# A first expert layer whose weights become the loaded operand, in a decoder layer on one core

## The reference

```python
for e in range(E):                                   # E = 4 experts, F = 512
    g = silu(einsum('bsd,fd->bsf', hidden_states, Wg[e]))
    u = einsum('bsd,fd->bsf', hidden_states, Wu[e])
    y = einsum('bsf,df->bsd', g * u, Wd[e])
    out = where((expert_ids == e)[..., None], y, out)
```

## Time and profile before

| what | value |
|---|---|
| median of 3 runs | 975.06 us (973.46 to 976.2) |
| profiled execution, its own time | 981.35 us |
| its span | 979.6 us |
| TensorE products / operand loads | 916.6 us busy / 517.6 us busy |
| VectorE, ScalarE, GpSimd busy | 698.2, 616.4, 325.2 us |
| expert and quantised stage | from 733.7 us to the end |

### The profile page before, as it was taken

How to read it: one execution, slowest core, us unless ns; L and a number is a source line. 1 busy time by engine, 2 the same in 40 slices (tenths; PEclk the granted TensorE clock), 3 DMA queues, 4 the chain that set the end, 5 groups by cost and what they waited for, 6 DMA issues and landing times.

```text
span 979.6 us, 19017 instructions
## 1 busy us (share of the span) xinstructions
PE 916.6 (94%) x6525; PEld 517.6 (53%) x6540; DVE 698.2 (71%) x1533; ACT 616.4 (63%) x1570; POOL 325.2 (33%) x450
## 2 busy tenths in 40 slices
PE   3899999999999999999999999999949899999974
PEld 2366676556556655655656556566414344444331
DVE  6799978778876778777667766776543378777672
ACT  3777778677777766776767667664102279887552
POOL 3477867123231422433242222301330012322211
PEclk9899999999999999999999999999978999999998
DMA  9636546676975534655454434459859977444343
GB/s 245 156 87 138 119 98 121 161 187 180 194 183 162 131 96 110 137 131 114 100 104 107 108 98 124 98 134 191 205 145 190 185 136 146 97 98 97 76 107 87
DMA packets 305631, 131.86 MB, mean 135 GB/s; under 512 B 275264, under 2 KB 279872, under 8 KB 305536
## 3 DMA queue, kind: packets, MB, share of 16 engines
q1 hardware_dynamic: 301616, 117.77, 56.0%
q0 software_dynamic: 3920, 12.86, 3.9%
HBM read 42.76 MB, written 20.99 MB: 65 GB/s over the span
## 4 chain that ended last, share of the span: by engine, by line
PE 82%; DMA 4%; DVE 3%; SPq 2%; issue 2%; ACT 2%; POOL 0%; DVEq 0%; ACTq 0%; POOLq 0%
PE S L250 7%; PE S L252 7%; PE S L251 7%; PE O L596 6%; PE QB L250 6%; PE QB L251 6%; PE QB L252 6%; PE O L594 5%; PE O L598 5%; PE OUTB L250 5%; PE OUTB L251 5%; PE OUTB L252 5%; PE OUTB L714 4%; PE S L698 4%; DMA P<-QTOKR 2%
## 5 line engine op out<-in xcount | busy, mean ns | idle before, releaser
L596 PE MATMUL O<-V,P 128*128 128x128 f16 x1024 | 179.1, 221 | 0.0
L594 PE MATMUL O<-V,P 128*128 128x129 f16 x1024 | 179.0, 219 | 0.1
L598 PE MATMUL O<-V,P 128*128 128x129 f16 x1024 | 178.9, 218 | 0.0
L1134 DVE CAST P<-P 128x1024 bf16<-128x1024 f32 x128 | 92.5, 723 | 113.5 <-ACT P L813 113.4
L1136 DVE TENSOR_TENSOR P<-P 128x1024 f16<-128x1024 f32 x128 | 161.0, 1258 | 4.4
L813 ACT ACTIVATE P<-S,cst 128x1024 f32<-128x1024 f32 x128 | 142.6, 1114 | 27.6 <-PE S L252 27.6
L1461 POOL TENSOR_SCALAR qst<-qs 128x4 f32<-128x4 f32 x64 | 14.2, 221 | 348.9 <-ACT junk L796 348.9
L796 ACT ACTIVATE junk<-QB 128x128 bf16<-128x128 f32 x208 | 54.6, 277 | 103.3 <-PE QB L252 103.3
L824 ACT ACTIVATE OTOK<-O,rd 128x128 f16<-128x128 f32 x256 | 80.5, 375 | 40.7 <-DVE rd L1141 40.0
L596 PEld LDWEIGHTS O<-V,P 128*128 128x128 bf16 x1024 | 99.2, 97 | 7.3
L594 PEld LDWEIGHTS O<-V,P 128*128 128x128 bf16 x1024 | 98.5, 96 | 7.9 <-DVE P L1136 0.6
(11 more groups left out here) (225 smaller groups left out, 1957.2 us busy)
## 6 DMA issues: line engine op xcount, KB each, us to landing
SIDE<-in_L_ffn_w_dram SPq DMA_DIRECT2D x64, 256.0 KB, 3.2
OTA<-sorted_rows SPq DMA_DIRECT2D x4, 1028.0 KB, 7.7
OTA<-in_L_attn_Wq_dram SPq DMA_DIRECT2D x4, 1024.0 KB, 6.9
SIDE<-in_L_attn_Wout_dram SPq DMA_DIRECT2D x16, 256.0 KB, 3.4
SIDE<-in_ctx_dram SPq DMA_DIRECT2D x16, 256.0 KB
ctx_split<-SIDE SPq DMA_DIRECT2D x16, 256.0 KB, 3.1
ROWB<-in_x_dram SPq DMA_DIRECT2D x16, 256.0 KB, 3.2
w_tern<-SIDE SPq DMA_DIRECT2D x32, 128.0 KB, 3.0
```

Source lines behind the costliest of these rows:

```text
L594: nc.tensor.matmul(o, ph(g)[:, a:a + P], V[:, b % 2, j, 0:129], start=j == 0, stop=False)
L596: nc.tensor.matmul(o[:, 0:128], ph(g)[:, a:a + P], V[:, b % 2, j, 130:258], start=False, stop=False)
L598: last = nc.tensor.matmul(o, pl(g)[:, a:a + P], V[:, b % 2, j, 0:129], start=False, stop=j == NT - 1)
L1134: nc.vector.tensor_copy(ph(g)[:, cols], P32[:, cols]).then_inc(p_hi, 1)
```

## The change

up() swaps the operands: a block of 128 features of the expert's weights is the loaded operand, and the tile's 128 turned rows are streamed past it. The product comes out with features on partitions and tokens in columns, block f in columns f * 128 of the same half of O. The gated values are then written straight to GT, and turn_gated, GHL and the semaphores gt fall away. gated_high now waits for the down() that read its part of GT four pairs ago (y_ps), and down() waits for gated_low (gu_lo).

```diff
-        GHL = (QTOKR[:, 0, :], QTOKR[:, 1, :])
...
-            def turn_gated(j):
-                sp.wait_ge(gu_lo, j + 1)
-                if j >= 4:
-                    sp.wait_ge(y_ps, j - 3)
-                sp.dma_start_transpose(GT[:, j % 4, :].rearrange("p (a n) -> p a n", n=P),
-                                       GHL[j % 2]).then_inc(gt[j % 4], 16)
-
...
-                if j < PAIRS:
-                    turn_gated(j)
...
+            def expert_block(e, s_, c, f):
+                return CT[:, bass.ds(e * 4096 + (s_ * DC + c) * F + f * P, P)]
+
+
             def up(j):
...
-                for c in range(DC):
-                    lhs = [HT[:, bass.ds(t * 1024 + (s_ * DC + c) * P, P)] for s_ in range(2)]
-                    last = split_products(O[:, (j % 2) * 512:(j % 2 + 1) * 512], lhs[0], lhs[1],
-                                          expert_rows(e, 0, c), expert_rows(e, 1, c), c == 0, c == DC - 1)
+                for f in range(F // P):
+                    for c in range(DC):
+                        rows = [HT[:, bass.ds(t * 1024 + (s_ * DC + c) * P, P)] for s_ in range(2)]
+                        a = (j % 2) * 512 + f * P
+                        last = split_products(O[:, a:a + P], expert_block(e, 0, c, f), expert_block(e, 1, c, f),
+                                              rows[0], rows[1], c == 0, c == DC - 1)
                 last.then_inc(z_ps, 1)
 
             def down(j):
                 e = pe.value_load(table[0:1, bass.ds(j, 1)], min_val=0, max_val=E - 1)
-                pe.wait_ge(gt[j % 4], (j // 4 + 1) * 16)
+                pe.wait_ge(gu_lo, j + 1)
...
             def gated_high(j):
                 act.wait_ge(gu, j + 1)
-                if j >= 2:
-                    act.wait_ge(gt[j % 4 - 2], ((j - 2) // 4 + 1) * 16)
-                nc.scalar.activation(GHL[j % 2][:, 0:F].bitcast(BF16), GU[j % 2], ACT.Copy
-                                     ).then_inc(gu_hi, 1)
+                if j >= 4:
+                    act.wait_ge(y_ps, j - 3)
+                nc.scalar.activation(GT[:, j % 4, 0:F].bitcast(BF16), GU[j % 2], ACT.Copy).then_inc(gu_hi, 1)
...
             def gated_low(j):
                 dve.wait_ge(gu_hi, j + 1)
-                nc.vector.tensor_tensor(GHL[j % 2][:, F:2 * F], GU[j % 2],
-                                        GHL[j % 2][:, 0:F].bitcast(BF16), ALU.subtract).then_inc(gu_lo, 1)
+                nc.vector.tensor_tensor(GT[:, j % 4, F:2 * F], GU[j % 2], GT[:, j % 4, 0:F].bitcast(BF16),
+                                        ALU.subtract).then_inc(gu_lo, 1)
```

More of the change, by code:

```diff
@@ L176, in decoder_layer @@
             "z_ps", "silu", "gu", "gu_hi", "gu_lo", "y_ps", "mask", "x3")
-        gt = sems("gt0", "gt1", "gt2", "gt3")
         (fmv, f_rs, f_nm, fx, fclip, f127, f_s1, fround, xq) = sems(
```

## The result

The changed kernel has a median of 1007.92 us over 4 runs (1007.31 to 1012.25), the kernel before, beside it on the same chip, 975.63 (973.46 to 977.39, 4 runs): ratio 1.0318, 95% interval 1.0288 to 1.0348, **slower**. The profiled execution took 1012.25 us, its span is 1010.4; before it was 981.35 and 979.6. So the trace has 30.8 us more to explain, and the prediction's sum had 25.4.

A forecast was written before the change was run, and what follows sets the result against it. TensorE was taken as the bound, with its sequencer pacing the changed up(). 16.4 us in slots 0 to 9 plus 9.0 in slots 10 to 18 made 25.4, giving 1000 us from a 975.06 median, range 988 to 1012.

The forecast's parts named there:

- First term: Slots 0 to 9, before hidden(0): the sequencer paces up() and down(), hidden(0) loads at 807 instead of 790.5, +16.4 us.
- the time of up() in the sequencer: A changed up(): 4.60 us of address steps plus 1.3 us of table loads, 5.90 us against 2.75 in the array.
- 6.5 us of waits: TensorE's waits before down() in the first stretch, taken to vanish with the removed transfer and counted within the +16.4 us.
- The interval of 0.124 us: Ordinary distance of address instructions in TensorE's sequencer, read from an up() of the kernel before.
- Second term: Slots 10 to 18: down() begins 1.0 us late in each of nine slots behind up()'s address steps, +9.0 us.
- time from loads to first step: Slots 10 to 18: from up()'s table loads to its first address step, taken as 1.9 us over the slots.
- The lead of 16 products: Slots 10 to 18: the sequencer is held some 16 products ahead of the array, so down() begins 1.0 us late.
- The distance of small products: In the array, 128-column products with own loads come every 0.0573 us, so up() takes 2.75 instead of 2.59 us.
- Half clock: Rival, first stretch: the clock stays at or falls to 1.2 GHz, slots of 10.2 us, +17, 1017 us; 7%.
- Hidden or faster steps: Rival: address steps are hidden and faster than before, the array alone counts, 969.5 us; 5%.
- A deeper lead: Rival, slots 10 to 18: the sequencer is further ahead than 16 products, 993 us; 5%.
- No change but in the array: Rival: other waits hold slots 3 to 8, steps are hidden, only 3 us of array stay, 978 us; 3%.

The follow-up runs named there:

- E1: Changed kernel with up()'s weights and rows at fixed addresses, so its 48 products have no address instruction: 976.18 us, ratio 0.9983 to the kernel before.
- e3: Changed kernel with up()'s weights at fixed addresses, rows still at loaded ones, 8 address instructions in an up(): 976.74 us, ratio 0.9997 to the kernel before.
- e4: Changed kernel with only the low half of up()'s weights at a fixed address, 20 address instructions: 981.46 us, ratio 1.0032 to the kernel before.
- e6: Kernel before with only the changed up() of 48 products put in, transfer kept: 1008.63 us, ratio 1.0316 to the kernel before.
- e5: Changed kernel with up() of the kernel before (12 products) put back, so only the transfer is removed: 974.34 us, ratio 0.997 to the kernel before.
- e8: Changed kernel with the expert's number kept from up() for down() instead of loaded again: 998.39 us, ratio 1.0218 to the kernel before.
- e10: Changed kernel with hidden(j-9) moved ahead of down(j-3) and the expert's number kept for down(): 996.21 us, ratio 1.0177 to the kernel before.
- e7: Kernel before with four turned loads of the second ternary weight issued in slots 6 to 9 instead of 2 to 5: 973.93 us, ratio 0.9959.

## Why the prediction was right, and where its sizes were off

**Direction and mechanism: right, and shown.** 36 address instructions make up() sequencer-bound, the array waits, and the removed transfer gives nothing back. E1, e3 and e4 show the first by number, e6 the second to 0.01 us. The time, 1007.92, is in the range and 8 us above the figure. The medians of one chip are 32.3 us apart and the spans of the two traces 30.8, where the sum had 25.4: 5.4 us are terms that were too small, and they are sized below. The other 2.5 are the scatter of the runs that the medians are made of (before's lie between 973.46 and 977.39 here, and up to 982.33 beside later kernels), and rounding. How much a term was too small hangs on the trace of before that it is held against, too: against the second one the first stretch lost 22.2 us and not 19.5.

**First term, 16.4, measured 19.5** (20.4 with 0.9 us that came from ahead of the stage: its first table load is at 734.7 instead of 733.8). The mis-sized quantity is the time of up() in the sequencer, 5.90, measured 6.15; ten of them make 2.5 us, and seven down() of 1.85 instead of 1.80 some 0.3, 2.8 of the 3.1 that were missing. One reading of the wait was wrong without harm to the sum: it gave all 6.5 us of waits to the transfer, and e5 shows that 2.9 remain without it. The interval of 0.124 us had been read where it was undisturbed. In the changed kernel it is still 0.124 at most steps and slips now and then to 0.18 to 0.28; by the slots of e4 and of the changed kernel it averages 0.13. Over 36 steps that is 0.2 us. What makes a step slip is open.

**Second term, 9.0, measured 10.5.** The forecast time from loads to first step, 1.9 us, had taken the long table loads of the earlier trace rows as an average. They come in alternate slots. Up()'s first table load of the changed kernel, in the slots from 857 and from 883 us, and the gelu on ScalarE at that time:
```profile
L657 PEldq TENSOR_LOAD <-table x1: 997/997/997, 860.3 to 860.3; - x1
...
L657 PEldq TENSOR_LOAD <-table x1: 1009/1009/1009, 886.7 to 886.7; - x1
```
```profile
860.08 1.11 ACT L980 ACTIVATE WOA<-S,fs 128x1024 f32<-128x1024 f32 x1
...
886.57 1.11 ACT L980 ACTIVATE WOA<-S,fs 128x1024 f32<-128x1024 f32 x1
```
The slots with a load of 0.92 to 1.01 us are 13.44 to 13.79 us long, those with 0.30 to 0.53 are 12.96 to 13.04. Four long ones at 0.5 us each are 2 us; without them the term would be 8.5. The two hidden-only slots cost 1.0 each, as forecast. Where the idle lies was told a little wrong. Between products there are 0.66 us ahead of down() instead of 0.8 (5.9 us over nine, the rest of the wait row above being in the first stretch; the 0.78 shown above is between operand loads, where 0.12 stand in before too). The remainder is within the last products of up().

**The lead of 16 products: held.** The gap ahead of down() is there in all nine slots, and goes when 16 fixed products stand ahead of down(). The Trainium skill (TensorE: Matmul & The Clock Gate, section on the array's architectural detail) has a queue 64 deep. By an estimate from that figure the second term would have been 1.5 us, and the trace disagrees with it, with 10.5 us and the lead of 16 read above.

**The distance of small products: held.** Without address instructions e1_fixed needs no more than before plus 0.97 us over nine slots, 0.11 each, against 0.16 forecast: its products start 0.056 us apart. The Trainium skill (TensorE: Matmul & The Clock Gate, section Back-to-back issue gap) has 81 ns. By an estimate from it the slots would have been 1.3 us longer each (48 by 0.081, less 2.59), and the trace disagrees, with 0.11.

**Rivals.** Half clock: its price is refuted, the granted clock of the first stretch is 0.94 against 0.92 before, and 1.00 in the second. But it did fall once on the way, as it does in before behind the wait of 3.56 us. Granted clock of after (the column before the last two), 744 to 748 us, in slot 1:
```profile
744.00:748.00 4.00, 3.99 (x39) 3.75 (x38) 0.32 (x1) 0.00 (x0) 0.00 (x0) 0.57 1.09 172
```
That cost nothing that the stretch shows: e6 has two such falls, from 745 and from 752 us, and is within 0.01 us of the changed kernel. Hidden or faster steps: refuted by e4 and the changed kernel, 0.13 each. A deeper lead: refuted by the gaps and by e8. No change but in the array: refuted, though its idea was half right. In the kernels that lack the address instructions, the wait for the vector engine's rows (2.6 to 2.9 us) does hold the last slots of the first stretch, which is part of why e1 and e5 gained less than forecast.

## What to carry to other kernels

Before a product is cut into smaller ones with operands at run-time addresses, count the address instructions that stand ahead of them and hold their sum against the array's time: here 36 at 0.13 us stood against 2.7 us of array. Where the addresses can be fixed, all of the loss goes (e1, e3, and nearly so e4). Where they can't, one number kept instead of loaded again takes a third of it back (e8: the ratio falls from 1.0318 to 1.0218), and that with fixed work between the two dynamic parts somewhat under half (e10: 1.0177). And ask of a transfer that is waited for what is queued around it: moving other loads to later slots (e7, 0.9959) won as much as removing it did (e5, 0.997; their intervals overlap).

## What the runs showed of the hardware

- Most address instructions are 46 ns long in the trace, yet one comes every 0.124 us at most steps and every 0.13 on average; products between them cost the sequencer nothing that can be seen.
- A table load on TensorE's sequencer takes 0.30 us in the first stretch (0.50 the first of all), and up to 1.01 in late slots. Three of the four long ones of the changed kernel begin 0.1 to 0.2 us after a gelu of ScalarE and end within 0.15 us of its end. The fourth does not fit: it begins at 833.43 and takes 0.92, and the gelu begins at 833.94. Nor does a load at 900.15, 0.62 us into a gelu, that took 0.31. VectorE's sum of rows (L1336) ran during each of the four as well. Neither was tested; the cause is open.
- Two executions of one kernel can differ by 2.7 us in a stretch of 55 that has waits in it, and by less than 0.3 in one of 102 that the array fills. In the first the granted clock differed too, 0.5 for 3.5 us more behind a wait of 3.56 us.
- TensorE's sequencer was 16 products ahead of the array in seven late slots of each of two kernels, with 0.20 us between the table load that follows and the operand load.
